# Softmax sums in attention: one TensorE total for some groups of four steps, their pair sums added by GpSimd, with more score slots and a longer score lead

## The reference, cut to what matters

```python
scores = jnp.einsum('bhqd,bhkd->bhqk', Q, K) / jnp.sqrt(jnp.float32(D_HEAD))
causal = jnp.tril(jnp.ones((n_ctx, n_ctx), dtype=bool))
scores = jnp.where(causal, scores, jnp.float32(-jnp.inf))
A = jax.nn.softmax(scores, axis=-1)
AV = jnp.einsum('bhqk,bhkd->bhqd', A, V)
```

## Time and profile before

| | us |
|---|---|
| median of 3 runs | 2518.35 |
| the profiled execution, its own time | 2517.91 |
| its span, first to last instruction | 2516.1 |
| attention of batch 0, first weigh to last total | about 748 to 1232 |
| attention of batch 1 | about 1427 to 1911 |

### The profile page before, as it was taken

How to read it: one execution, slowest core, us unless ns; L and a number is a source line. 1 busy time by engine, 2 the same in 40 slices (tenths; PEclk the granted TensorE clock), 3 DMA queues, 4 the chain that set the end, 5 groups by cost and what they waited for, 6 DMA issues and landing times.

```text
span 2516.1 us, 40155 instructions
## 1 busy us (share of the span) xinstructions
PE 2446.6 (97%) x14559; PEld 1069.2 (42%) x14559; DVE 1760.5 (70%) x2956; ACT 1476.7 (59%) x2827; POOL 1537.3 (61%) x1596
## 2 busy tenths in 40 slices
PE   6999999999999999999999999999999999999998
PEld 3444444444443433333344433434334444444443
DVE  8866666667669695957676786868576766666665
ACT  7766666665225656566532356565674566666665
POOL 5577776664325677677322367676873566776775
PEclk9999999999999999999999999999999999999999
DMA  2122111121122111000420312020006101111101
GB/s 69 34 84 87 57 38 39 42 101 68 34 61 63 31 29 40 20 21 4 151 84 23 92 27 55 6 53 6 20 4 219 58 26 43 51 51 51 51 34 51
DMA packets 78117, 130.61 MB, mean 52 GB/s; under 512 B 19647, under 2 KB 24794, under 8 KB 77790
## 3 DMA queue, kind: packets, MB, share of 16 engines
q1 hardware_dynamic: 77918, 128.05, 16.6%
HBM read 68.23 MB, written 31.46 MB: 40 GB/s over the span
## 4 chain that ended last, share of the span: by engine, by line
PE 78%; DVE 9%; POOL 7%; ACT 2%; issue 2%; SPq 2%; DMA 1%; POOLq 0%; DVEq 0%; ACTq 0%
PE pp L97 59%; PE ps L97 17%; POOL sb L106 6%; DVE sb L118 3%; DVE sb L112 3%; ACT sb L103 2%; SPq L139 2%; PE ps L100 1%; DVE sb L106 1%; POOL sb L109 1%; DVE sb L109 1%; PE pp L100 1%; DMA sb<-sb 0%; DVE sb L115 0%; DVE sb L136 0%
## 5 line engine op out<-in xcount | busy, mean ns | idle before, releaser
L97 PE MATMUL pp<-sb,sb 128*128 128x512 f16 (+7 forms) x11230 | 2055.9, 420 | 20.3 <-DVE sb L112 9.6
L106 POOL TENSOR_TENSOR sb<-sb,sb 128x512 f32<-128x512 f32 (+6 forms) x1345 | 1484.3, 1130 | 947.7 <-ACT sb L103 317.6
L97 PEld LDWEIGHTS pp<-sb,sb 128*128 128x128 f16 (+3 forms) x11230 | 776.3, 101 | 1048.3 <-issue 234.1
L97 PE MATMUL ps<-sb,sb 128*128 128x512 f16 (+7 forms) x2786 | 720.6, 347 | 20.5 <-DVE sb L112 10.5
L103 ACT ACTIVATE sb<-pp 128x512 f32<-128x512 f32 (+7 forms) x1018 | 515.9, 549 | 284.3 <-PE pp L97 272.8
L118 DVE TENSOR_REDUCE sb<-pp 128x1 f32<-128x512 f32 (+2 forms) x720 | 452.6, 666 | 191.6 <-PE pp L97 189.0
L103 ACT ACTIVATE sb<-sb 128x512 f16<-128x512 f32 (+4 forms) x513 | 326.0, 649 | 351.2 <-DVE sb L112 293.4
L112 DVE SCALAR_TENSOR_TENSOR sb<-pp,sb,sb 128x512 f32<-128x512 f32 x447 | 324.5, 746 | 149.2 <-PE pp L97 133.5
L112 DVE SCALAR_TENSOR_TENSOR sb<-ps,sb,sb 128x512 f32<-128x512 f32 x437 | 318.2, 746 | 155.6 <-PE ps L97 128.5
L97 PEld LDWEIGHTS ps<-sb,sb 128*128 128x128 f16 (+3 forms) x2786 | 254.4, 98 | 341.0 <-DVE sb L118 36.0
L103 ACT ACTIVATE sb<-ps 128x512 f32<-128x512 f32 (+5 forms) x490 | 270.3, 558 | 151.3 <-PE ps L97 121.3
(11 more groups left out here) (29 smaller groups left out, 365.6 us busy)
## 6 DMA issues: line engine op xcount, KB each, us to landing
sb<-sb SPq DMA_DIRECT2D x144, 128.0 KB, 2.4
sb<-L_attn_X SPq DMA_DIRECT2D x64, 256.0 KB, 3.4
sb<-xa SPq DMA_DIRECT2D x64, 256.0 KB, 4.4
sb<-xc SPq DMA_DIRECT2D x64, 256.0 KB, 3.5
xa<-sb SPq DMA_DIRECT2D x32, 256.0 KB, 2.0
xc<-sb SPq DMA_DIRECT2D x32, 256.0 KB, 4.3
out<-sb SPq DMA_DIRECT2D x32, 256.0 KB, 2.0
sb<-sb SPq DMA_DIRECT2D x48, 96.0 KB, 2.1
```

Source lines behind the costliest of these rows:

```text
L97: return self.e.matmul(*a, **k) if self.e else self
L106: return self.e.tensor_tensor(*a, **k) if self.e else self
```

## The change

Some groups of four steps, held in `whole` by their last step, get a single total. For these GpSimd adds the two pair sums once more, in `add_pairs`: four adds, one for each head, of the width of the second pair. The total then runs over all 512 queries. A group is taken as whole by the planner after its second weigh, if it begins at step 16 or later, if the late phase has not begun, and if the planned clock of GpSimd is not past that of TensorE. 16 of the 40 groups of a batch are whole.

The order in `line` becomes weigh k, weigh k+1, weigh k+2, total of the group before, weigh k+3; a group that isn't whole gets a total of its first pair right behind that one. The slot of the first step of a whole group is held until its one total, that of the third until the second addition. Two E slots are added: seven from step 48, eight from step 88, six again from 120. The bound of the score lead is 4m+8 plus 11 heads at all times (before, 3 while maxima are left, else 7), where m is the next step to be weighed. The planner's constants change, the time it books for a turn between modes from 100 ns to 0 among them.

```diff
--- before.py
+++ after.py
@@ -1323,7 +1323,7 @@
         self.p = p
         o = QS0 + 65536
         self.E = [p.at([128, 4, 512], F32, x) for x in [o + 8192 * i for i in range(NE)] +
-                  [QS0 + 98304, QS0 + 106496, C0, C0 + 8192]]
+                  [QS0 + 98304, QS0 + 106496, C0, C0 + 8192, C0 + 16384, C0 + 24576]]
         o = KP0 + 16384
         self.rec = p.at([128, 512], F32, o)
         self.sums = p.at([128, 512], F32, o + 4096)
@@ -1342,9 +1342,9 @@
             p.sign("a_" + x) for x in names)
         self.steps = [(hg, qt, kt) for hg in range(4) for qt in range(4) for kt in range(4 * qt + 4)]
         self.banks = [Banks() for _ in range(B)]
-        self.late = [set() for _ in range(B)]
+        self.late, self.whole = [set() for _ in range(B)], [set() for _ in range(B)]
         self.slots = {}
-        self.late_added = p.sign("a_late_added")
+        self.late_added, self.summed = p.sign("a_late_added"), p.sign("a_summed")
         self.plan = [list(self.order(b)) for b in range(B)]
 
     def offset(self, n):
@@ -1429,23 +1429,27 @@
         exped, weigh_end, sum_end, kept, inverted, added = {}, {}, {}, 0.0, -1e9, {}
         red_end = 0.0
         total_units, total_scores = len(units), 4 * N
-        m, hold = 0, [None] * 8
+        m, hold = 0, [None] * 10
 
         def released(k):
             if k is None:
                 return 0.0
+            last = k - k % 4 + 3
             if k % 2:
                 return max(added[k], weigh_end[k]) if k in added else None
+            if last in self.whole[b]:
+                return summed.get(last) if k % 4 else sum_end.get(last)
             return sum_end.get(k + 1)
 
         def pick(n):
-            most = range(NE) if n < 16 else (0, 1, 2, 3, 6, 7) if n < 120 else range(6)
+            most = range(NE) if n < 16 else (0, 1, 2, 3, 6, 7, 8, 9)[:6 + (n >= 48) + (n >= 88)] if n < 120 else range(6)
             known = [(released(hold[i]), i) for i in most if released(hold[i]) is not None]
             return min(known) if known else None
 
         late, mode, where = False, "row", 0
-        line = [x for k in range(0, N, 2) for x in
-                [("total", k - 1) if x == "T" else ("weigh", k + int(x)) for x in '0T1'] if x[1] >= 0]
+        line = [x for k in range(0, N, 4) for x in
+                [("total", k - 1) if x == "T" else ("weigh", k + int(x)) for x in '012T3'] if x[1] >= 0]
+        summed = {}
         while line:
             n, j = scored
             free = n < N and (j or pick(n))
@@ -1456,31 +1460,31 @@
             head = units[0][0][0] if units else None
             first = 4 * n + j < 4 * m + 8
             cand = []
-            if ready and 4 * n + j < 4 * m + 8 + (7 if wide else 3):
+            if ready and 4 * n + j < 4 * m + 8 + (11 if wide else 11):
                 hunger = max(act - pe, 0)
-                cand.append((max(pe, clear[i], rowed[steps[n][0:2]]) + 0.050000 * hunger + (0 if first else 300.000000), "score", i))
+                cand.append((max(pe, clear[i], rowed[steps[n][0:2]]) + 0.073110 * hunger + (0 if first else 361.700000), "score", i))
             if head == "max":
                 at, x = 4 * units[0][0][1] + units[0][0][2], steps[min(n, N - 1)]
                 if at <= 4 * x[0] + x[1] + 2 and (lead < 9.000000 or not cand):
-                    hunger = max(dve - pe, 0) + 6272.000000 * (lead - 0.096000)
-                    cand.append((max(pe, clear[i]) + 0.050000 * hunger, "max", i))
+                    hunger = max(dve - pe, 0) + 3486.000000 * (lead - 0.091240)
+                    cand.append((max(pe, clear[i]) + 0.073110 * hunger, "max", i))
             elif head == "rows":
                 cand.append((max(pe, low_at, clear[i]) - (500 if low_at <= pe else 0), "rows", i))
             elif head:
                 cand.append((pe - 9e9, head, 0))
             op, k = line[0]
-            can = k in added if op == "total" else 4 * n + j >= 4 * k + 4
+            can = k in (summed if k in self.whole[b] else added) if op == "total" else 4 * n + j >= 4 * k + 4
             if can:
-                ok = (max(added[k], inverted if steps[k][2] == 1 else 0.0) if op == "total" else
+                ok = (max(summed.get(k, 0.0), added[k], inverted if steps[k][2] <= 3 else 0.0) if op == "total" else
                       max(exped[k, 3], kept if steps[k][2] == 0 else 0.0))
-                begin = max(ok, pe + (100.000000 if mode == "row" else 0))
-                cand.append((begin + (300.000000 - 0.200000 * min(max(dve - pe, 0), 2000) - 0.000000 * min(max(act - pe, 0), 2000)
+                begin = max(ok, pe + (0.000000 if mode == "row" else 0))
+                cand.append((begin + (608.900000 - 0.321500 * min(max(dve - pe, 0), 2000) - 0.095840 * min(max(act - pe, 0), 2000)
                                       if mode == "row" else
-                                      0.000000 - 0.110000 * min(max(min(dve, act) - pe, 0), 2000)), "stay", 0))
+                                      82.440000 - 0.098800 * min(max(min(dve, act) - pe, 0), 2000)), "stay", 0))
             at, what, i = min(cand, key=lambda x: x[0])
             if what in ("score", "max", "rows"):
                 if mode == "col":
-                    pe, mode = pe + 100.000000, "row"
+                    pe, mode = pe + 0.000000, "row"
                 at = max(pe, clear[i], rowed[steps[n][0:2]] if what == "score" else low_at if what == "rows" else 0.0)
             if what == "stay":
                 seq = [line.pop(0)]
@@ -1489,7 +1493,7 @@
                 elif k == 119:
                     seq.append(("wo", None))
                 if mode == "row":
-                    pe += 100.000000
+                    pe += 0.000000
                 mode = "col"
             else:
                 seq = ((what, None),)
@@ -1557,9 +1561,16 @@
                   pe = at + 4 * c / 2.4 + 20
                   weigh_end[n] = pe + 235
                   out.append(("weigh", n))
+                  if n % 4 == 1:
+                      if n >= 17 and not late and pool <= pe + 0.000000:
+                          self.whole[b].add(n + 2)
+                      else:
+                          line.insert(2, ("total", n))
                   if n % 2:
                       work, start = 4 * c, max(weigh_end[n - 1], exped[n, 3])
-                      if late and n >= late or max(dve, start) + 1.04 * work + 1000000000.000000 < max(pool, start) + 2.117 * work:
+                      if n - n % 4 + 3 in self.whole[b]:
+                          pass
+                      elif late and n >= late or max(dve, start) + 1.04 * work + 1000000000.000000 < max(pool, start) + 2.117 * work:
                           self.late[b].add(n)
                       for h in range(4):
                           start = max(weigh_end[n - 1], exped[n, h])
@@ -1569,20 +1580,22 @@
                           else:
                               pool = max(pool, start) + 2.117 * c + 141
                               added[n] = pool + 110
+                  if n in self.whole[b]:
+                      pool += 4 * (2.117 * (512 - self.offset(n - 1)) + 141)
+                      summed[n] = pool + 110
                   if steps[n][2] == 4 * steps[n][1] + 3:
                       act = max(act, weigh_end[n]) + 479
                       kept = act + 180
               elif what == "total":
                   n = step
-                  c = 512 - self.offset(n - 1)
-                  at = max(pe, added[n], inverted if steps[n][2] == 1 else 0.0)
+                  c = 512 - (0 if n in self.whole[b] else self.offset(n - 1))
+                  at = max(pe, summed.get(n, 0.0), added[n], inverted if steps[n][2] <= 3 else 0.0)
                   pe = at + 4 * c / 2.4 + 20
                   sum_end[n] = pe + 235
                   self.sum_up(out, parts, n)
                   if parts and parts[0][0] == "invert" and steps[n][2] == 4 * steps[n][1] + 3:
                       inverted = max(dve, sum_end[n]) + 745
-        for k in range(N - 2 + 1, N, 2):
-            self.sum_up(out, parts, k)
+        self.sum_up(out, parts, N - 1)
         yield from out
         yield from parts
 
@@ -1695,13 +1708,18 @@
         elif what == "total":
             n = at[0]
             hg, qt, kt = t.steps[n]
-            off, last = t.offset(n - 1), kt == 4 * qt + 3
-            if kt == 1 and n > 1:
-                e.wait_ge(*t.inverted.at((b, *t.steps[n - 2][0:2], 0)))
-            e.wait_ge(*(t.late_added.at((b, n, 1)) if n in t.late[b] else t.e_added.at((b, n, 3))))
+            last, whole = kt == 4 * qt + 3, n in t.whole[b]
+            first, back = kt == (3 if whole else 1), 3 if whole else 1
+            off = 0 if whole else t.offset(n - 1)
+            if first and n > 3:
+                e.wait_ge(*t.inverted.at((b, *t.steps[n - back - 1][0:2], 0)))
+            if whole:
+                e.wait_ge(*t.summed.at((b, n, 3)))
+            else:
```

(19 more changed lines are left out.)

## The result

The changed kernel takes 2526.32 us (median of 5 runs, 2525.02 to 2527.49) beside 2517.96 for the kernel before: a ratio of 1.003, 95% interval 1.002 to 1.0041. It is 8.4 us slower. I had forecast 2491.0 with 2512 as the upper end, so the sign was wrong.

The account below looks back on a forecast made before the run. TensorE's matmul queue was taken as the bound. Dropped totals (-23.3 us), fewer turns (-7.2) and added waits (+3.2) summed to -27.3 us, giving 2491.0 us against the median, range 2468 to 2512.

Parts of the forecast that it names:

- What bounds the kernel: Both attentions: TensorE's matmul queue bounds, busy 97% of the span, so a dropped matmul saves its pitch.
- rival D: TensorE is not the bound and dropped totals only leave gaps: 2518 us; chance 0.06 together with Rival B in full.
- the reading by weight-load share: TensorE's weight-load busy share of 38% means much headroom, so dropped matmuls could gain nought.
- Part 1: Whole groups' single totals on TensorE: 11 full and 5 diagonal groups save 11.7 us a batch, 23.3 in both.
- Part 4: Longer lead, slots and constants: 15 fewer runs of weighs and totals, saving 3.6 us a batch, 7.2 in both.
- the lower bound of this term: Least gain from fewer turns between row and column modes: no fewer runs at all, 0 us.
- my signs of being wrong: GpSimd waits reaching 10 us a batch, TensorE idle in steps 16 to 47 with ScalarE late, or runs under 100.
- Parts 2 and 3: GpSimd's added adds, mostly hidden, and the new order's late totals: 1.6 us a batch, 3.2 in both.
- Rival B: GpSimd becomes the bound in stretches without maxima, cancelling the gain: 2518 us; in full 0.06 together with rival D.
- part 3: New order: second totals at query-block ends wait for VectorE's transposition, 0.6 us a batch.
- Rival A: E slots held longer make ScalarE wait and TensorE run dry: 2537 us; chance in full 0.08.
- Rival C: The longer lead does much more: 45 fewer runs of weighs and totals, 2476.6 us; chance 0.20.

Follow-up runs that it names:

- Experiment 7: Version of experiment 5 with a second set of matmuls, as wide as the dropped total, after each whole group's total; 2540.31 us, ratio 1.0087.
- experiment 1: Kernel before with only the change's new planner constants, no whole groups, new slots or longer lead; 2547.25 us, ratio 1.0115.
- Experiment 2: Changed kernel with all planner constants as before; whole groups, eight slots, line order and lead kept; 2530.22 us, ratio 1.0048.
- experiment 5: Changed kernel, same written order, GpSimd's second addition cut to 2 columns, sums bounded below by 1; 2519.21 us, ratio 0.9999.
- experiment 6: Version of experiment 2 with GpSimd's second addition cut to 2 columns and sums bounded below by 1; 2512.46 us, ratio 0.9971.
- experiment 4: Kernel before with only eight E slots and the score bound of 11 heads; 2519.83 us, ratio 1.0005.
- experiment 8: Changed kernel with other planner constants (turn 50 ns), lead limits 5 and 9, 17 whole groups, 119 runs of weighs and totals; 2506.31 us, ratio 0.9954.
- Experiment 3: Changed kernel without whole groups, and no query block's first total before the last one's inversion; 2629.53 us, ratio 1.0438.

## Why the prediction was wrong

**What bounds the kernel: right.** Experiment 7 moved nothing but totals in TensorE's queue and found 21 to 22 us for 22.5. With that, rival D falls, and so does the reading by weight-load share (the Trainium skill, Perfetto Trace Analysis, "Identifying the Most-Contended Engine"): loads are busy 36% of the changed attention (175.68 of 489 us), and still each dropped total paid.

**Part 1, dropped totals: right.** 10 full and 6 diagonal groups give 11.2 us a batch by the prediction's pitches, for my 11.7, and experiment 7 bears the price out.

**Part 4, turns: wrong, and the largest miss.** I booked 15 runs fewer; there are 34 more. At the 0.27 us of experiment 1 that is 18.4 us slower instead of 7.2 faster, some 26 us out of the 35 between forecast and result (at the 0.23 us of the pitches below, 15.6 us and some 23). The step that failed was my reading of the planner's constants. I had taken "staying in column mode now costs 82" as one more reason to expect little, and the turn booked at nothing as harmless. `order` is plain Python, and its written order can be counted with one constant changed at a time (no run on the chip):

| planner's constants, one batch | runs of weighs and totals |
|---|---|
| kernel before | 143 |
| before, only the turn booked at 0 | 160 |
| before, only the price for staying 82.44 - 0.0988 x backlog | 197 |
| before, all the new ones (experiment 1) | 197 |
| before, all the new ones but the price for staying | 154 |
| changed kernel | 177 |
| changed kernel, old booking of the turn | 165 |
| changed kernel, old price for staying | 157 |

So it is the price for staying above all. At nothing, the smallest backlog of the other engines let the next weigh win against a score at hand. At 82 it takes more (480 ns, if the planned clocks of VectorE and ScalarE stand equally far past TensorE's), so the planner often leaves after one weigh: 146 single pieces. The turn at nothing adds to it. No single constant was timed by itself. I had set the lower bound of this term at no change, without a reason that excludes a loss, and none of my signs of being wrong looked for more runs. The price of a turn was near enough (0.24 by the rows, 0.23 by all pitches, 0.27 at most by experiment 1).

This step alone didn't turn the sign. Experiment 2 has 7 runs more than the kernel before in place of 34, and is slower still.

**Parts 2 and 3, waits: mis-sized.** I booked 3.2 us. GpSimd's busy time was right (389 for 388 us), but the work wasn't hidden: its cost is 7.1 to 8.4 us (experiment 5), and 17.8 to 19.0 us where the constants of before are kept (experiment 6). Rival B was the right mechanism, at the place it named, and weighed too low: GpSimd was already unbroken for 20.30 us in the stretches without maxima, and the adds of whole groups taken just ahead of them now reach in. In the first such stretch it is busy all the time, where the earlier trace rows had 18.31 us:

```profile
848.00:869.00 21.00, 20.85 (x150) 6.57 (x151) 5.62 (x10) 17.63 (x36) 21.00 (x18) 1.00 0.02 6
```

The planner's clock for GpSimd, on which the choice of groups rests, adds only the sums; the scalings and splits that stand in the same queue aren't in it. That this is what makes it choose too many groups is only argued. The wait that part 3 named, for VectorE's transposition (L136), hardly grew: TensorE's loads wait 1.1 us for it in the first attention, and 0.9 before. What the new order costs besides, the later row matmuls of experiment 6, I had booked nowhere.

**The account.** For both batches, each run beside its own kernel before: turns +18.4, totals -21.8, GpSimd +8.4 make +5.0 of the measured +8.4. The remaining 3.4 us are no more than the intervals leave open (about 2.5 to 4 us for each of these runs). The parts aren't independent either. With the constants of before, turns and totals by the same prices would put experiment 6 some 18 us under the kernel before, and it is 6.8 under; and there the same kind of groups cost GpSimd waits of 17.8 us, perhaps since a faster TensorE comes to each total earlier.

**Rival A** (slots) is hardly seen: experiment 4 gives no difference, and ScalarE waits for GpSimd 3.9 us in all (2 times) in the changed attention. **Rival C** (fewer turns) was the right lever, in a direction that this change didn't take; experiment 8 did.

## What to carry to other kernels

When a planner's prices are changed, count the pieces that it then writes before forecasting: the order is known without a run, and 177 for 143 would have set the sign of this term. Try each constant alone, since the one that does the harm (a small price for staying) may look the least. Work moved to an engine that is 66% busy in its stage is free only where that engine has gaps (GpSimd had 165 us of them in each attention, but none in the stretch of the earlier trace rows); read the stretches where it is unbroken, since the mean hides them. Work taken out of an order is worth its pitch only if the rest doesn't come later. A bound of nought on a term needs a reason just as a price does.

## What the runs showed of the hardware

**A turn between column and row matmuls costs 0.23 us for the round trip by pitch, and 0.27 us with its waits** (29.2 us for 108 of them, experiment 1), at 128 x 32 float32 against 128 x 128 and 96 x 128 float16. The pitch sums three steps, start to start, as medians of the first attention before. Leaving: from the last matmul of a pass of 512 columns to a row matmul it is 525 ns, against 409 to the next pass. Entering: from a row matmul of 512 columns it is 309 ns, against 219 to another row matmul. And the first pass in the column mode lasts 433 ns, the later ones 409. All are the same in the changed kernel and in experiment 1. The Trainium skill (TensorEngine Tiling (Array Packing), section "Key Properties") says that changing the tiling mode drains TensorE; that agrees, and the price is from here.

**Short falls of the granted clock take part in such losses.** The same three windows, first in the changed kernel, then in the kernel before:

```profile
789.00:793.00 4.00, 4.00 (x13) 1.12 (x16) 3.06 (x5) 3.39 (x7) 0.00 (x0) 0.57 0.00 0
1147.00:1151.00 4.00, 3.08 (x17) 1.08 (x17) 2.45 (x5) 3.89 (x8) 4.00 (x4) 0.58 0.02 4
1188.00:1192.00 4.00, 4.00 (x21) 0.68 (x14) 1.89 (x3) 0.00 (x0) 4.00 (x4) 0.57 0.00 0
```

```profile
789.00:793.00 4.00, 4.00 (x22) 1.10 (x21) 3.16 (x6) 3.45 (x8) 1.16 (x1) 1.00 0.00 0
1147.00:1151.00 4.00, 2.93 (x24) 1.05 (x22) 3.23 (x6) 3.90 (x8) 3.00 (x3) 1.00 0.09 25
1188.00:1192.00 4.00, 4.00 (x42) 1.67 (x38) 1.17 (x3) 2.21 (x6) 2.18 (x2) 1.00 0.02 4
```

A window mean of 0.57 is a stretch mostly at the lower of the two levels, 1.2 GHz; (1 - 0.57) x 4 us is 1.7 us lost in each. The third follows directly on the 2.2 us wait for GpSimd, so a wait can be paid nearly twice. It isn't always so: experiment 2's longest wait, 2.7 us at 1194, has a granted clock of 1.00 for all of 1190 to 1200. The second window lies at a spot where TensorE was short of work in both kernels (3.08 and 2.93 of 4 us busy), and only the changed one was slowed, so such a fall isn't to be told from the wait beside it alone. In its two attentions the changed kernel has five falls, the kernel before one. These are the others, in the changed kernel (two) and in the kernel before (one):

```profile
1470.00:1476.00 6.00, 4.62 (x15) 1.39 (x19) 4.87 (x9) 4.08 (x8) 0.00 (x0) 0.72 0.02 5
1870.00:1876.00 6.00, 5.83 (x31) 1.72 (x32) 2.47 (x4) 1.02 (x3) 5.01 (x5) 0.72 0.00 0
```

```profile
1464.00:1470.00 6.00, 4.81 (x19) 1.39 (x19) 4.81 (x8) 4.25 (x8) 0.00 (x0) 0.72 0.02 5
```

The one at 1870 stands behind the same wait for GpSimd, of 2.23 us again, in the second attention. Over all executions the mean granted clock is 0.9956 in the changed kernel (five), 0.9973 in experiment 5 (ten) and 0.9972 in the kernel before beside it (sixteen). By that, an estimate, about 4 of the 7 to 8 us that GpSimd's additions cost are time at the lower level. Experiment 3 is the far end of this, with a mean of 0.57 over 27 us.
